# Second mixture of experts: from every expert for every token to blocks of each token's two chosen experts

## The chip, the cores and the metric

The kernel runs on one core of one Trainium2 chip. The metric is the device time of one execution in microseconds (us); the time of a kernel is the median of its runs. A profiled execution, which carries the trace, is a run of its own.

## The reference, cut to what matters

Two transformer layers, each an attention and a mixture of experts, over `x` of 16 rows x 256 tokens x 128 features in float32. After each of the four parts stands `x = layernorm(x + part(x))`. The change touches the last part alone:

```python
def _L1_ffn_ref(x, router_w, w1, w2):        # E = 8 experts, K = 2, H = 512
    logits = einsum('bsd,ed->bse', x, router_w)
    topk_vals, topk_idx = top_k(softmax(logits), K)
    for eid in range(e):
        w = sum(where(idx == eid, vals, 0), axis=-1)
        h = gelu(x_flat @ w1[eid].T)
        y = h @ w2[eid].T
        out = out + w[:, None] * y
```

The weight `w` is zero for the six experts that a token didn't choose. The first layer's mixture (8 experts of 256 and a shared one) has the same form and stays as it is.

## The kernel before

One row (256 tokens, two tiles of 128) is the unit of work. The program is a software pipeline over 18 iterations. Iteration `it` computes stage a of row `it` (first attention, first mixture's up products), stage b of row `it - 1` (first mixture's down products, second attention, router and up products of the second mixture) and stage c of row `it - 2` (gates, down products of the second mixture, last normalization, output). Iterations 0 and 1 and 15 to 17 are written out; 2 to 14 are one hardware loop (`run`, `FIRST`, `LAST`). All weights lie in SBUF from the start. Products that need precision are split in two float32r halves, three products each (`products`).

An iteration has two halves. First the head loop, eight steps `s` of two heads: scores (`score_pair`), their maxima on VectorE (`head_max`, L652), exponent on ScalarE (`softmax_exp`, L544), transposition on TensorE, copy, product with the values, scaling. Then the rest: the output product `OUT`, values of the next row `V0` to `V3`, the transposed row `X1T`, the up products `U0_*` of the first mixture, the end of the second attention (`AOT`, `PROJ`, `X3T`), the next row's `QK0`, `QK1`, and the up products of the second mixture.

The order on TensorE is written by hand in `pe_units(it)`, a list of units with the PSUM bank of each; rings of two or four banks are used in turn. `FILL_B` and `FILL_C` place units of stages b and c between the steps of the head loop. Each unit waits until its bank is drained, and each drain until it is filled. The other engines have their own orders: `body` under `block.scalar`, `block.vector`, `block.gpsimd` and `block.sync`. All engines execute in order.

What the change touches, in its present form:

- `U1_0` to `U1_15` (TensorE, L969 to L971 and L1086) with `gelu1` (ScalarE, L572): x3T times `w1` of every expert, six experts in three split products, two in whole float32. They end the iteration on TensorE; ScalarE loads the exponent's table only behind the last of them.
- `D1e0` to `D1e7` (TensorE, L1101) with `mix` (VectorE, L731): each expert's 512x128 down product, then `x4 = x4 + gate * y`. Six of them stand in the head loop, two behind `OUT`.
- `gate(v, 1, 2)`, `ln_stats` and `ln_apply` of `x4`, and the store of `x4`, all for row `it - 2`.
- `up1`, `up1_whole`, `down1` (SBUF weights, loaded by SyncE) and `split_up_weights(4, ...)` on GpSimd in iteration 0.
- GpSimd's order in an iteration: `rms`, `inverse_std` 1, `head_product`, `value_product`, `inverse_std` 0, 3, 2, `plus`. `plus` frees `x_row`, whose next load SyncE issues at the start of the next iteration; ScalarE squares it at step 1 of the head loop.

## Time and profile before

| | us |
|---|---|
| median of 3 runs (1561.91 to 1562.41) | 1562.2 |
| profiled execution, its own time | 1567.07 |
| its span, first to last instruction | 1565.3 |
| busy: TensorE / VectorE / ScalarE / GpSimd | 1421.9 / 985.5 / 860.9 / 514.5 |
| mean granted TensorE clock, of 1 | 0.976 |

Busy times are sums over instructions. Matmuls are pipelined: each record lasts about 0.28 us while the next starts after 0.12, so the time between starts says what one costs. A product of two whole float32 operands makes two records. The profile's line numbers are those of the kernel above.

### The profile page before, as it was taken

To read this page: it belongs to the slowest core of one execution; us is meant where nothing else is said; L and a number is where in the kernel's file an instruction comes from. 1 tells how busy PE (TensorE), PEld (TensorE's weight loads), DVE (VectorE), ACT (ScalarE), POOL (GpSimd) and SP (SyncE) were. 2 spreads that over 40 slices of the span, in tenths; PEclk is the share of its full clock that TensorE was granted. 3 is DMA by queue.
4 is the path that set the end of the run, shared out by engine and by line. 5 is a ranking of instruction groups with operands and counts; after the bars stand their busy time and mean duration, and the time that the engine had idled before them with its cause. 6 is when DMAs were issued, how large, how long until landed. Compare 5 with 4: busy or idle time off the path is not lost.

```text
span 1565.3 us, 34497 instructions
## 1 busy us (share of the span) xinstructions
PE 1421.9 (91%) x12096; PEld 1249.4 (80%) x12096; DVE 985.5 (63%) x2534; ACT 860.9 (55%) x2361; POOL 514.5 (33%) x415
## 2 busy tenths in 40 slices
PE   6897999999999999999999999999999999998847
PEld 5675888888888888878888888888888887887747
DVE  4456576675757667575666757667575766757482
ACT  5564655656465564647556464655646465463403
POOL 3206061340605134060522506043250614315040
PEclk9898999999999999999999999999999999998978
DMA  7000000000000000000000000000000000000000
GB/s 239 4 2 1 5 2 8 0 7 0 0 7 0 7 0 7 0 0 7 0 7 0 7 0 0 7 0 7 0 1 5 0 7 0 3 1 1 4 1 7
DMA packets 14088, 13.78 MB, mean 9 GB/s; under 512 B 1625, under 2 KB 12770, under 8 KB 13794
## 3 DMA queue, kind: packets, MB, share of 16 engines
q1 hardware_dynamic: 14050, 13.27, 2.6%
q8 instruction: 24, 0.39, 0.1%
q14 instruction: 14, 0.11, 0.0%
HBM read 11.17 MB, written 2.10 MB: 8 GB/s over the span
## 4 chain that ended last, share of the span: by engine, by line
issue 62%; POOL 17%; POOLq 14%; PE 4%; DVE 1%; ACT 1%; DMA 0%; DVEq 0%; SPq 0%
POOLq L329 8%; POOL hid L466 6%; POOL hid L471 6%; POOLq L473 5%; POOL std_inv L427 2%; PE bank_F L1101 1%; POOL up_lo L436 1%; POOL x L488 1%; POOL x_plus L450 1%; POOL rms_inv L443 1%; PE bank_S L983 0%; DMA b_out<-in_b_out 0%; ACT probs L544 0%; DVE hid L743 0%; DVE hid L761 0%
## 5 line engine op out<-in xcount | busy, mean ns | idle before, releaser
L1101 PE MATMUL bank_F<-down,hid 128*128 128x128 f32 x3072 | 374.9, 278 | 34.6 <-DVE x L731 34.0
L1101 PEld LDWEIGHTS bank_F<-down,hid 128*128 128x128 f32 x3072 | 359.4, 193 | 46.3 <-DVE x L731 38.1
L544 ACT ACTIVATE probs<-bank_S,neg_max 128x256 f32<-128x256 f32 x512 | 235.5, 475 | 179.0 <-DVE neg_max L652 178.9
L652 DVE TENSOR_REDUCE neg_max<-bank_S 128x2 f32<-128x512 f32 x256 | 164.6, 684 | 83.5 <-PE bank_S L983 80.2
L471 POOL TENSOR_TENSOR hid<-hid,qkv 128x1024 f32<-128x1024 f32 x62 | 177.1, 2857 | 47.1 <-ACT hid L560 47.1
L731 DVE SCALAR_TENSOR_TENSOR x<-bank_F,gates,x 128x128 f32<-128x128 f32 x512 | 155.2, 345 | 31.6 <-PE bank_F L1101 21.4
L523 ACT ACTIVATE probsT<-bank_T 128x512 f32<-128x512 f32 x256 | 139.6, 605 | 44.1 <-PE bank_T L1012 44.0
L426 POOL TENSOR_TENSOR var_eps<-mv,ln_eps 128x2 f32<-128x2 f32 x64 | 12.5, 195 | 428.5 <-DVE mv L690 428.5
L441 POOL TENSOR_TENSOR mean_sq<-sum_sq,one_over_d 128x2 f32<-128x2 f32 x16 | 3.1, 194 | 455.1 <-ACT h_row L518 455.1
L1012 PE MATMUL bank_T<-ident,probs 128*128 128x128 f32 x1024 | 138.4, 279 | 0.1
L459 POOL TENSOR_TENSOR hid<-qkv 128x1024 f32<-128x1024 f32 x47 | 112.2, 2386 | 66.6 <-ACT qkv L523 66.6
L1040 PE MATMUL bank_A<-probsT,values 128*64 128x256 f32 x1024 | 133.5, 382 | 0.4 <-ACT probsT L523 0.4
L1012 PEld LDWEIGHTS bank_T<-ident,probs 128*128 128x128 f32 x1024 | 113.8, 142 | 23.4 <-issue 21.3
L572 ACT ACTIVATE hid<-bank_T 128x512 f32<-128x512 f32 x141 | 84.2, 598 | 75.5 <-PE bank_T L971 60.4
L466 POOL TENSOR_TENSOR hid<-hid 128x512 f32<-128x512 f32 x77 | 112.8, 1465 | 10.9
L969 PE MATMUL bank_T<-x1T_hi,up_lo 128*128 128x256 f32 x378 | 114.4, 303 | 0.4
L665 DVE TENSOR_TENSOR oT<-oT,bank_A 128x256 f32<-128x256 f32 x128 | 53.6, 419 | 97.0 <-ACT oT L532 95.9
L971 PE MATMUL bank_T<-x1T_hi,up_hi 128*128 128x256 f32 x378 | 107.8, 285 | 0.0
L970 PE MATMUL bank_T<-x1T_lo,up_hi 128*128 128x256 f32 x378 | 107.8, 285 | 0.0
L544 ACT ACTIVATION_READ_ACCUMULATOR probs<-bank_S,neg_max 128x1 f32 x512 | 105.9, 207 | 0.0
L983 PE MATMUL bank_S<-qk_hi,qk_lo 64*128 64x256 f32 x512 | 86.5, 333 | 17.1 <-ACT probs L544 12.5
L572 ACT ACTIVATE hid<-bank_F 128x512 f32<-128x512 f32 x115 | 68.7, 598 | 50.4 <-PE bank_F L971 33.7
(167 smaller groups left out, 3259.1 us busy)
## 6 DMA issues: line engine op xcount, KB each, us to landing
x_row<-in_x SPq DMA_DIRECT2D x16, 128.0 KB, 2.1
down<-in_w SPq DMA_DIRECT2D x1, 2048.0 KB, 14.0
out<-x SPq DMA_DIRECT2D x16, 128.0 KB, 1.8
hid<-in_w SPq DMA_DIRECT2D x1, 1536.0 KB, 7.8
hid<-in_rw SPq DMA_DIRECT2D x1, 1024.0 KB, 6.6
hid<-in_wv SPq DMA_DIRECT2D x1, 512.0 KB, 3.8
hid<-in_wq SPq DMA_DIRECT2D x1, 512.0 KB, 4.7
hid<-in_wk SPq DMA_DIRECT2D x1, 512.0 KB, 5.6
```

The source lines that it names most:

```text
L329: eng.drain()
L466: return g.tensor_tensor(x[:, :, :, 0:n // 2], x[:, :, :, 0:n // 2], x[:, :, :, n // 2:n], ALU.add)
L471: ins = g.tensor_tensor(pv1[:, t, half(i)], *weights_and_values(t, i), ALU.mult)
L523: sc.activation(dst, src, ACT.Copy).then_inc(v.drain(name)[0], 1)
L544: ins = sc.activation(probs[:, h // 2 % 2, h % 2, t, :], unit.bank(f"S{h}")[:, t * S:(t + 1) * S], ACT.Exp, bias=neg_max[:, h, t:t + 1], a ...
L572: sc.activation(hid1[:, e, m:m + 2, :], v.bank(f"U1_{u}")[:, :].rearrange("p (m n) -> p m n", m=2), ACT.Gelu).then_inc(v.drain(f"U1_{u}")[ ...
L652: ve.tensor_reduce(neg_max[:, h, :], v.bank(f"S{h}")[:, :].rearrange("p (t k) -> p t k", t=NT), AX.X, ALU.max, negate=True).then_inc(max_r ...
L731: ins = ve.scalar_tensor_tensor(acc[:, t, :], y[:, j, t, :], gates[i][:, t, e:e + 1], src[:, t, :], ALU.mult, ALU.add)
L969: te.matmul(out, s_lo, m_hi, start=True, stop=False)
L1012: ins = te.transpose(bank[:, k * S + t * P:k * S + (t + 1) * P], probs[:, h // 2 % 2, h % 2, t, tokens(k)], ident[:])
L1040: ins = te.matmul(bank[r, 0:S], values[:, k, s * P + j * DH:s * P + j * DH + DH], probsT[:, j, k, :], start=k == 0, stop=k == NT - 1)
L1101: ins = te.matmul(bank[:, (j * NT + t) * P:(j * NT + t + 1) * P], hid[:, e, k, tokens(t)], down[:, e, k, :], start=k == 0, stop=k == m - 1)
```

## The change

What it does: the second mixture is computed for each token's two chosen experts alone. Rows are taken in five groups (0 to 3, 4 to 7, 8 to 11, 12 to 14, 15). TensorE counts, with a triangular product (`RK`), at which place of its expert each token stands; `place_row` makes two slot numbers of it, and GpSimd scatters the token's normalized features (`x3`) to those two slots of a DRAM buffer `xs[g]`, which has a region of blocks of 128 places for each expert and was filled with zeros. Once the last row of a group is counted (`CN`), `map_blocks` writes on one partition which blocks are used and of which expert: at most 4 x rows + 7 blocks, 23, 19 or 11 a group, and always so many are computed. SyncE reads place and expert of each block into registers and loads the block (64 KB), the expert's `w1` (256 KB) and `w2` (256 KB) into one of eight slots. A block is transposed (`XT`), multiplied with `w1` (`UB`, whole float32), passed through gelu, multiplied with `w2` (`DB`), and stored to its place in `xs[g]`. Once all blocks of a group are stored GpSimd gathers each token's two results, and `combine` adds them to `x3` with their gates; statistics, normalization and store follow. Blocks go in waves (`WAVES`: group, first block, count, iteration of the up product, iteration of the down product). The program is written out whole: no hardware loop.

In the up products nothing is split any more, and `x3` keeps ten rows. The diff, cut to its core:

```diff
-FILL_C = {(2, 1): ["D1e0"], (4, 1): ["D1e1"], (5, 1): ["D1e2"], (6, 1): ["D1e3"], (7, 0): ["D1e4"], (7, 1): ["D1e5"]}
+GROUPS = [range(0, 4), range(4, 8), range(8, 12), range(12, 15), range(15, 16)]
+WAVE_SIZES = [(0, 5, [6, 6, 6, 5]), (1, 9, [6, 6, 6, 5]), (2, 13, [8, 8, 7])]
+WAVES = [(g, sum(sizes[:i]), n, first + i, first + i + 1) for g, first, sizes in WAVE_SIZES for i, n in enumerate(sizes)]
+WAVES += [(3, 0, 8, 16, 16), (3, 8, 8, 16, 16), (3, 16, 3, 16, 16), (4, 0, 8, 17, 17), (4, 8, 3, 17, 17)]
+GATHERS = {9: [0, 1], 10: [2, 3], 13: [4, 5], 14: [6, 7]}
+DOWN_PLACES = [(2, 1), (4, 1), (5, 1), (6, 1)]
...
# fill_units: RK at (0, 0) of stage c, CN at (1, 0) of a group's map iteration,
# DB units at DOWN_PLACES (from iteration 16 on all at (3, 1), then the first XT)
...
# pe_units, iterations of stage a
+        put("F", *[name for w in waves for name, _ in transpose_units(w)])
         put("A", "V0", on=nxt)
         put("G", "V1", on=nxt)
         put("A", "V2", on=nxt)
+        put("G", *blocks[:2])
         put("A", "X1T")
...
         put("A", "V3", on=nxt)
+        put("G", *blocks[2:3])
         put("G", "X3T", on=b)
         put("A", "QK0", "QK1", on=nxt)
+        put("G", *blocks[3:4])
         put("G", "R1", on=b)
+        put("G", *blocks[4:5])
         put("S0", "S0", on=nxt)
         put("S1", "S1", on=nxt)
+        put("G", *blocks[5:])
...
# pe_units, iterations 16 and 17
+    put("G", *up0, *xt1)
+    for i, name in enumerate(dn0):
+        put("G", name, *up1[2 * i:2 * i + 2])
+    if it == ROWS:
+        put("G", "AOT", *xt2, *dn1[:2], *up2, "PROJ", *dn1[2:], "X3T", "R1", *dn2)
+    else:
+        put("G", *dn1)
...
# SyncE
+            def load_blocks(w):
+                g, first, n, up, _ = WAVES[w]
+                if first == 0:
+                    sp.wait_ge(map_ready, g + 1)
+                    sp.wait_ge(scattered[g], 16 * 2 * NT * len(GROUPS[g]))
+                for j in range(n):
+                    place = sp.value_load(block_map[0:1, g, 0, first + j:first + j + 1], ...)
+                    expert = sp.value_load(block_map[0:1, g, 1, first + j:first + j + 1], ...)
+                    # waits until slot j's last block is transposed
+                    sp.dma_start(xb[:, j, :], xs[g][bass.ds(place, 1), :, :]...).then_inc(xb_in[j], 16)
+                for j in range(n):
+                    # waits until slot j's last up product is done
+                    sp.dma_start(w1b[:, j, :], w1_in[bass.ds(expert, 1), :, :]...).then_inc(w1_loaded[j], 16)
...
+                for w in waves_up(v.it):   # in body, behind load_x and zero_fill
+                    load_blocks(w)
+                    if w:
+                        store_blocks(w - 1)
+                    load_down(w)
+                for row in GATHERS.get(v.it - 1, []):
+                    store_row(row)
...
# GpSimd: scatter(row it - 2) ahead of rms; gather(rows) ahead of plus; four each
+            def scatter(v, row):
+                for t in range(NT):
+                    for c in range(2):
+                        g.indirect_dma_start(xs[i]..., bass.IndirectOffsetOnAxis(ap=slots_of[:, row, t, c:c + 1], axis=0),
+                                             x3[:, row % X3_ROWS, t, :], None).then_inc(scattered[i], 16)
...
# VectorE, head loop: place_row at step 0, map_blocks at step 1, gate_row behind gate(v, 1, 2),
# combine(rows gathered in the iteration before) at step 2, combine_norm at step 3
+            def place_row(v):     # nine small instructions
+            def gate_row(v):      # five
+            def map_blocks(v):    # twelve, on one partition
+            def combine(rows):
+                for row in rows:
+                    dve.wait_ge(gathered[i], 16 * 2 * NT * (row // 2 + 1))
+                    for c in range(2):
+                        for t in range(NT):
+                            ins = ve.scalar_tensor_tensor(x[:, t, :], yg[:, i, t, c, :], gates_of[:, row, t, c:c + 1], x[:, t, :], ...)
+                    ln_stats(3 + i, x)
...
# run
-            with eng.Fori(0, LAST - FIRST + 1) as step:
-                body(Iteration(FIRST, step, banks))
+            for it in range(ROWS + 2):
+                body(iteration(it))
```

In iteration 16 ScalarE passes the first wave's blocks through gelu ahead of the second attention's exponent, and VectorE copies that wave's transposed blocks ahead of the second attention's products; the two halves of `gather` for rows 8 to 11 stand between GpSimd's products.

## Rows read from the trace of the kernel before

**Rows 1.** The page: busy time of TensorE; DMA share in 40 slices.
```profile
PE 1421.9 (91%) x12096; PEld 1249.4 (80%) x12096; DVE 985.5 (63%) x2534; ACT 860.9 (55%) x2361; POOL 514.5 (33%) x415
...
DMA  7000000000000000000000000000000000000000
```

**Rows 2.** Timeline of ScalarE, table loads: start us, us, instruction.
```profile
83.09 1.28 ACT L556 ACT_TABLE_LOAD   x1
...
176.84 1.28 ACT L556 ACT_TABLE_LOAD   x1
...
729.76 1.28 ACT L556 ACT_TABLE_LOAD   x1
...
821.93 1.28 ACT L556 ACT_TABLE_LOAD   x1
...
1470.32 1.28 ACT L556 ACT_TABLE_LOAD   x1
```

**Rows 3.** Busy time by stretch: us, PE PEld DVE ACT POOL, granted clock, DMA.
```profile
83.10:175.20 92.10, 77.96 (x643) 66.31 (x644) 58.63 (x147) 52.05 (x144) 30.59 (x23) 0.94 0.01 3
...
639.50:731.70 92.20, 87.12 (x759) 76.78 (x758) 60.37 (x159) 53.23 (x149) 31.65 (x25) 1.00 0.01 3
...
1470.30:1545.00 74.70, 47.55 (x309) 42.78 (x307) 45.52 (x96) 15.26 (x28) 19.78 (x13) 0.79 0.01 2
```

**Rows 4.** Timeline of TensorE, steady iteration.
```profile
715.39 0.36 PE L969 MATMUL bank_T<-x1T_hi,up_lo 128*128 128x256 f32 x1
...
728.95 3.73 PE L1101 MATMUL bank_F<-down,hid 128*128 128x128 f32 x32
...
763.71 1.95 PE L1101 MATMUL bank_F<-down,hid 128*128 128x128 f32 x16
...
765.58 0.39 PE L983 MATMUL bank_S<-qk_hi,qk_lo 64*128 64x256 f32 x2
...
794.85 0.44 PE L953 MATMUL bank_A<-ident,x 128*128 128x128 f32 x2 [1.55 <-DVE x L696]
```

**Rows 5.** Timeline of VectorE, steady iteration.
```profile
734.34 1.29 DVE L652 TENSOR_REDUCE neg_max<-bank_S 128x2 f32<-128x512 f32 x2 [0.57 <-PE bank_S L983]
...
789.06 0.42 DVE L800 TENSOR_TENSOR x<-bank_A,x_plus 128x256 f32<-128x256 f32 x1 [2.37 <-PE bank_A L1025]
...
814.13 1.29 DVE L652 TENSOR_REDUCE neg_max<-bank_S 128x2 f32<-128x512 f32 x2
...
826.50 1.29 DVE L652 TENSOR_REDUCE neg_max<-bank_S 128x2 f32<-128x512 f32 x2 [0.57 <-PE bank_S L983]
```

**Rows 6.** Timeline of VectorE, iteration 1.
```profile
87.39 1.28 DVE L652 TENSOR_REDUCE neg_max<-bank_S 128x2 f32<-128x512 f32 x2
...
91.12 1.29 DVE L652 TENSOR_REDUCE neg_max<-bank_S 128x2 f32<-128x512 f32 x2 [0.16 <-PE bank_S L983]
...
141.92 0.42 DVE L800 TENSOR_TENSOR x<-bank_A,x_plus 128x256 f32<-128x256 f32 x1 [2.44 <-PE bank_A L1025]
...
169.02 1.29 DVE L652 TENSOR_REDUCE neg_max<-bank_S 128x2 f32<-128x512 f32 x2 [0.25 <-PE bank_S L983]
```

**Rows 7.** Groups of instructions by line and form.
```profile
L731 DVE SCALAR_TENSOR_TENSOR x<-bank_F,gates,x 128x128 f32<-128x128 f32 x512 | 155.2, 345 | 31.6 <-PE bank_F L1101 21.4 <-issue 2.2
...
L716 DVE TENSOR_TENSOR marked<-marked,rexp 128x16 f32<-128x16 f32 x32 | 5.6, 175 | 2.4
```

**Rows 8.** SyncE's queue and the DMA list (KB, us to landing).
```profile
12.00 4.16 SPq L360 DMA_DIRECT2D down<-in_sw  x1
...
19.73 0.43 SPq L360 DMA_DIRECT2D down<-in_w  x1
...
x_row<-in_x SPq DMA_DIRECT2D x16, 128.0 KB, 2.1
```

**Rows 9.** Timeline of GpSimd, head sums in the head loop.
```profile
762.92 1.28 POOL L466 TENSOR_TENSOR hid<-hid 128x512 f32<-128x512 f32 x1
...
766.66 2.07 POOL L466 TENSOR_TENSOR hid<-hid 128x512 f32<-128x512 f32 x1
```

More of the change, by code:

```diff
@@ L30 @@
 F32R = mybir.dt.float32r
+I32 = mybir.dt.int32
 ALU = mybir.AluOpType
@@ L45, with n_blocks, region_blocks, space_blocks @@
 LN_EPS, RMS_EPS = 1e-5, 1e-6
-SPLIT1 = 6
-FIRST, LAST = 2, ROWS - 2
+GROUPS = [range(0, 4), range(4, 8), range(8, 12), range(12, 15), range(15, 16)]
+SLOTS = 8
+X3_ROWS = 10
+def n_blocks(g):
+    return 4 * len(GROUPS[g]) + E - 1
+def region_blocks(g):
+    return 2 * len(GROUPS[g])
+def space_blocks(g):
+    return -(-(E * region_blocks(g) + E - 1) // 8) * 8
+def group_of(row):
+    return [g for g, rows in enumerate(GROUPS) if row in rows][0]
+def map_iteration(g):
+    return GROUPS[g][-1] + 2
@@ new lines, in down_units, with up_names, unit_with, earlier @@
+def down_units(w):
+    n = WAVES[w][2]
+    return [(f"DB{w}_{i}", range(2 * i, min(2 * i + 2, n))) for i in range(-(-n // 2))]
+def up_names(w):
+    return [f"UB{w}_{j}" for j in range(WAVES[w][2])]
+def unit_with(units, j):
+    return [name for name, slots in units if j in slots][0]
+def earlier(w, j):
+    return [u for u in range(w) if WAVES[u][2] > j]
+def waves_up(it):
+    return [w for w, wave in enumerate(WAVES) if wave[3] == it]
+def waves_down(it):
+    return [w for w, wave in enumerate(WAVES) if wave[4] == it and wave[3] != it]
@@ new lines, in transformer_blocks @@
+        xb = sb("xb", P, SLOTS, D)
+        xbT = sb("xbT", P, SLOTS, P)
+        yb = sb("yb", P, SLOTS, D)
+        yg = sb("yg", P, 2, NT, 2, D)
+        projections = [w1b[:, 2 * n:2 * n + 2].rearrange("p a h -> p (a h)") for n in range(3)]
+        zeros = hidb[:, 0:2].rearrange("p a k s -> p (a k s)")
+        upper = sb("upper", P, P)
+        one = sb("one", P, 1)
+        first_slot = sb("first_slot", P, 1, E)
+        thresholds = sb("thresholds", 1, 1, MAX_REGION)
+        lower = sb("lower", 1, E, E)
@@ L611, in body @@
                     if v.b and s == 5:
+                        if not v.a:
+                            for j in range(WAVES[waves[0]][2]):
+                                gelu1(v, waves[0], j)
                         head_exp(v, 0)
@@ L617, in body @@
                 sc.activation(table_load[:], table_load[:], ACT.Gelu)
+                if not v.a:
+                    for w in waves[1 if v.b else 0:]:
+                        for j in range(WAVES[w][2]):
+                            gelu1(v, w, j)
+                    return
                 if v.next:
@@ new lines, in combine @@
+            def combine(rows):
+                for row in rows:
+                    i = row % 2
+                    dve.wait_ge(gathered[i], 16 * 2 * NT * (row // 2 + 1))
+                    x = x3[:, row % X3_ROWS]
+                    for c in range(2):
+                        for t in range(NT):
+                            ins = ve.scalar_tensor_tensor(x[:, t, :], yg[:, i, t, c, :], gates_of[:, row, t, c:c + 1], x[:, t, :],
+                                                          ALU.mult, ALU.add)
+                        settled(dve, ins)
+                    ln_stats(3 + i, x)
@@ L817, in fill_out, with combine_norm @@
+            def combine_norm(rows):
+                for row in rows:
+                    ln_apply(3 + row % 2, x3[:, row % X3_ROWS], row // 2 + 1)
             def fill_out(v, s, place):
                 for name in fill_units(v.it, s, place):
+                    if name == "RK":
+                        place_row(v)
+                    if name == "CN":
+                        map_blocks(v)
+                    if name[:2] == "XT":
+                        blocks_transposed(v, int(name[2:].split("_")[0]), [name])
+                    if name[:2] == "DB":
+                        blocks_out(v, int(name[2:].split("_")[0]), [name])
@@ L877, in body @@
                     residual(v, "OUT", x1, x_plus)
-                    ln_stats(v, 0, x1)
+                    ln_stats(0, x1)
+                    for w in waves:
+                        blocks_transposed(v, w)
                 if v.b:
@@ L922, in body @@
                     route(v, 1)
+                if not v.a:
+                    combine(GROUPS[2][2:])
+                    blocks_out(v, waves[2])
+                    combine_norm(GROUPS[2][2:])
                 if v.next:
```

480 lines of the change are left out of this document (364 added, 116 removed).

## The prediction

> **What bounds the kernel now.** I read the page first: TensorE is busy 91% of the span and the DMA engines are idle after the first slice [rows 1], so weights may be fetched again at little cost in the middle of the program. The table loads of ScalarE mark where each iteration begins its head loop [rows 2]: from 729.76 to 821.93 is one period, 92.17 us. The chain of waits is mostly "issue" and says little; the stretches say more. A steady iteration has TensorE busy 87.1 of 92.2 us and VectorE only 60.4 [rows 3]. That looks like a plain TensorE bound, and the second mixture is a large share of it: 64 down products of 128x128 an iteration are 128 records, and 16 records start to start take 765.58 - 763.71 = 1.87 us, 0.117 us each [rows 4], so 15.0 us. The up products are the stretch from 715.39 to 728.95 [rows 4], 13.6 us, of which some 1.4 belong to the router and the next scores.
>
> But one iteration shows how far that reading carries. Iteration 1 runs the head loop without any down unit of the second mixture, because no row is that far yet. TensorE is busy 78.0 us in it, not 87.1 [rows 3], and still the loop's starts lie 176.84 - 83.09 = 93.75 us apart [rows 2]. Read by stages on VectorE: from the first pair of maxima to the residual of the attention output takes 50.8 us there [rows 6], 54.7 in the steady state [rows 5]. So removing six down units (6 x 1.87 = 11.2 us of TensorE) shortens the loop by 3.9 us: the chain scores, maximum, exponent, transposition sets its pace. From the residual to the first maxima of the next row VectorE works nearly without a break, 25.1 us (27.1 in iteration 1, where the granted clock averages 0.94 [rows 3]). And from those maxima to the next loop it takes 12.4 us [rows 5], because ScalarE cannot load the exponent's table before the last up unit; at the start of iteration 1, with no up units ahead of it, the same step takes 3.7 us [rows 6].
>
> **Removed.** The three stages, one by one. The loop: six down units go, three of two blocks each come back (16 records each, as D1e had), in iterations 6 to 15. Half of 3.9 us: 50.8 + 2.0 = 52.8. The new place_row and gate_row add 14 small VectorE instructions, 0.175 us each [rows 7] and about 0.25 with their drains, 3.5 us; they stand in the first two steps of the loop, where VectorE partly waits for scores, and I charge 1.5. That makes 54.3. The second stage: the split copy of X3T and the statistics and normalization of x4 leave VectorE, the copies of the transposed blocks come, but TensorE has an up block ahead of X3T; 25.1 becomes 24.3. The third stage: of the 13.6 us of up products six blocks of 8 records (0.94 us each) remain, two of them ahead of X1T, where TensorE now waits 1.55 us for the normalization [rows 4], and the last one soon after the next scores. The exponent's table can then be loaded before the maxima are there: 3.7 us. The period is 54.3 + 24.3 + 3.7 = 82.3 us. Iterations 1 to 5 carry no down blocks, but may run partly at the lower clock as iteration 1 does; I give them the same. From the start of iteration 1 to that of iteration 16 is 1470.32 - 83.09 = 1387.2 us [rows 2]; 15 x 82.3 = 1234.5. That is -152.7.
>
> **Added inside the loop iterations.** The block map (12 small VectorE instructions in iterations 5, 9 and 13) blocks the queue ahead of the gates and D0p3: about 3.4 us each, of which I charge 2.7: 8 in all. Rows 0 to 7 are combined in iterations 10, 11, 14 and 15: four products of 0.345 us [rows 7] and about as much again in statistics and normalization, 2.8 us a row, of which I charge 2.0: 16. Together +24.
>
> The GpSimd queue: scatters (four indirect DMAs) stand ahead of rms and of the second normalization; gathers (eight in iterations 9, 10, 13, 14) ahead of plus, and so ahead of the next x_row load. No row shows an indirect DMA. Bounds are SyncE's issue, 0.43 us, and its longest, 4.16 [rows 8]. As each works over 128 rows on the same cores I take the nearest GpSimd row, 1.28 us [rows 9]. Scatter: 5.1 us, done about 11 us into the loop; rms waits for squares that come at about 13. Gathers: 10.2 us after the last normalization, when GpSimd is idle for nearly 20 us; plus and x_row (2.1 us [rows 8]) still land before ScalarE squares it. Cost nothing; without this cover, up to 4 x 10 us. The vector engine disturbs GpSimd: the same addition takes 1.28 us alone and 2.07 beside a product of VectorE [rows 9]. The Trainium skill, "SBUF — State Buffer", section "Who interferes with whom", says a DMA issued by GpSimd is starved of descriptors while VectorE copies in its two-port mode (620 ns become 3100 in its example); no run here shows that for a DMA yet, and by its figure a scatter would take some 12 us and be late for rms by about 5.
>
> Traffic: 99 blocks (23, 23, 23, 19 and 11) bring 64 + 256 + 256 KB each and store 64, and 296 places of 64 KB are zeroed in iterations 0 to 4. One x_row of 128 KB lands in 2.1 us [rows 8]; six blocks are 3.8 MB an iteration, some 12 to 20 us of 82 on idle engines [rows 1]. Hidden, as is the zeroing. The gone splitting of the up weights on GpSimd was hidden; the new constants there cost 1 us at the start.
>
> **Straight-line code.** Iteration 1 is already straight-line, and at 93.75 us it is no shorter than the loop's 92.17 [rows 2], which holds a back edge: nothing to win or lose is seen there, and I charge nothing. The Trainium skill, "Runtime: NRT & Kernel Launch", section "Instruction fetch mechanics", says that instructions are streamed in blocks ahead of use and that a taken branch breaks this; by it unrolling could only help, the trace shows no such gain.
>
> **The end.** This is where it gives back. Before, from 1470.32 to the end is 1565.3 - 1470.3 = 95.0 us. Now 30 of the 99 blocks are computed there, one dependent chain behind another, and SyncE's single queue serves them. An issue is 0.43 us [rows 8]; for reading a register from the map no row stands near but that same issue (bounds: nothing, and a DMA's 2.1 us). Per block two reads and four issues (x, w1, w2, store), 6 x 0.43 = 2.6 us; a wave of eight is 20.6 us, 10.3 of them before its last x block is asked for, and one of three 7.7. Walked through from the start of iteration 16: map ready at 12; first wave transposed at 30, behind seven down blocks; its up blocks and table loads put the second attention's exponent back by about 15 us; second wave landed at 47; its down and up blocks to 62; combine rows 8 and 9; AOT at 73, X3T at 84, the last down wave at 97, and only behind it RK of row 15. Then place and four scatters 8, landing 2, eight places read and loaded 12, the rest of SyncE's work and the last down blocks 31, stores 3, four gathers and landing 7, combine, norm and the output 7: 97 + 70 = 167. TensorE is granted 0.79 there already [rows 3]; 30 blocks at half clock would cost 57 us more, I charge 13. So 180 against 95: +85.
>
> **Sum.** -152.7 + 24 + 85 + 1 = -42.7 us against the profiled execution's 1567.07, that is 1524; the median runs are 0.31% below it, so 1520 us. Changes under 0.2% (3 us) can't be told from none.
>
> **Rivals.** (a) The forecast, 1495 to 1545: 0.50. (b) The price of places and row gates is fully hidden (15 x 1.5 = 22 us less) and SyncE's reads are near nothing (60 x 0.43 x 0.8 = 20 less): about 1478. For it: VectorE waits in just those steps; against: four engines take turns there. 0.22. (c) The other side: the end is set by register reads on SyncE. At 2.1 us each, 60 reads cost 60 x 1.67 x 0.8 = 80 us more: 1600. It decides against the change from 1562, that is from 1.3 us a read. For it: they stand in one queue with all loads and stores, nothing overtakes. Against: in waves one and two other waits hide part. 0.20. (d) The iterations gain only what TensorE's idle stages allow and the added DMAs, descriptor starvation or instruction supply costs 3 us in each: 1520 + 45 = 1565, no gain. For it: iteration 1 with 9 us less TensorE work took 93.75 us. Against: its long third stage was the up units, which go. 0.08.
>
> Faster: (a), (b) and part of (d) 0.75; within 0.2%: 0.03; slower: 0.22. The range takes in (b) and most of (c): 1468 to 1592; within (a) alone 1495 to 1545.
>
> **What would show it.** Table loads of the exponent about 82 us apart in iterations 2 to 15; if 88 or more, the third stage did not close. First maxima to the next loop in 4 us. SyncE's issue of eight places in about 10 us; if 20, (c). Iteration 16 and 17 together 180 us; TensorE with about 1,700 records less: a row's second mixture has 72 + 16 up and 128 down records, 3456 in all, against 99 x (1 + 8 + 8) = 1683 and a few for the ranks. The prediction is wrong above all if the walk through the end is off by half, or if the gathers delay x_row.

## The result, and the profile after

The changed kernel took 1616.3 us (median of four runs, 1612.1 to 1618.8) against 1562.3 us for the kernel before beside it: a ratio of 1.033, 95% interval 1.0315 to 1.0346. It is slower, where 1520 us were forecast. The profiled execution took 1612.05 us, its span is 1610.3.

One thing must be said before any row is read. The same program, measured again in three later sets, each beside the kernel before (1564 to 1566 us there), took 1575.2, 1575.8 and 1575.9 us, ratios of 1.005 to 1.007. So two results stand: slower by 3.3% once, by 0.5 to 0.7% three times. Both are slower than before, where faster was forecast. The 41 us between them are followed below, as far as the runs go; their cause stays open. "The control" is the first of the three later ones (experiment 5; its span is 1573.5 us).

The page of the first profile after: busy times and the granted clock in 40 slices; they answer to [rows 1].

```profile
PE 1291.1 (80%) x10473; PEld 1110.6 (69%) x10473; DVE 983.1 (61%) x2660; ACT 776.3 (48%) x2206; POOL 626.6 (39%) x550
PEclk9998998898799999999998888999998899887756
```

TensorE lost 131 us of busy time and 1,623 records, VectorE 2 us. The clock, a 9 almost throughout before, has 8s in the middle and ends at 5 and 6. It is 0.94 on average over iterations 1 to 15 of the control, where it was 0.99 before.

ScalarE's loads of the exponent's table in the first profile after, which answer to [rows 2]: the starts of iterations 1, 9, 10, 11, 12, 16 and 17.

```profile
75.61 1.28 ACT L817 ACT_TABLE_LOAD   x1
757.04 1.28 ACT L817 ACT_TABLE_LOAD   x1
849.91 1.28 ACT L817 ACT_TABLE_LOAD   x1
951.73 1.28 ACT L817 ACT_TABLE_LOAD   x1
1049.16 1.28 ACT L817 ACT_TABLE_LOAD   x1
1418.56 1.28 ACT L817 ACT_TABLE_LOAD   x1
1511.45 1.28 ACT L817 ACT_TABLE_LOAD   x1
```

And the same loads in the control:

```profile
77.66 1.28 ACT L817 ACT_TABLE_LOAD   x1
757.79 1.28 ACT L817 ACT_TABLE_LOAD   x1
845.42 1.28 ACT L817 ACT_TABLE_LOAD   x1
939.17 1.28 ACT L817 ACT_TABLE_LOAD   x1
1029.18 1.28 ACT L817 ACT_TABLE_LOAD   x1
1383.83 1.28 ACT L817 ACT_TABLE_LOAD   x1
1475.62 1.28 ACT L817 ACT_TABLE_LOAD   x1
```

The span falls into three parts, all read from such rows:

| us | before | forecast | first profile | control |
|---|---|---|---|---|
| start to iteration 1 | 83.1 | 84.1 | 75.6 | 77.7 |
| iterations 1 to 15 | 1387.2 | 1258.5 | 1343.0 | 1306.2 |
| iterations 16 and 17 | 95.0 | 180 | 191.7 | 189.7 |

The iterations gained 44 us in the first profile and 81 in the control, where 129 were forecast; the end cost 97 and 95 where 85 were. By the prediction's stages on VectorE, in us: the loop (from the first maxima inside it to the residual of the attention output), from there to the first maxima of the next row, and from those to the next loop's:

| iteration | forecast | first profile | control |
|---|---|---|---|
| 2 | 54.3 / 24.3 / 3.7 | 51.8 / 25.5 / 4.4 | 51.8 / 25.5 / 4.4 |
| 6 | same | 55.6 / 25.2 / 3.7 | 54.0 / 28.2 / 3.7 |
| 8 | same | 54.4 / 24.9 / 3.7 | 54.4 / 24.9 / 3.7 |
| 5 (map) | 57.0 / 24.3 / 3.7 | 59.9 / 24.9 / 4.0 | 59.4 / 24.8 / 4.0 |
| 9 (map, gather) | 57.0 / 24.3 / 3.7 | 57.5 / 28.6 / 6.6 | 57.0 / 24.9 / 4.0 |
| 10 (combine, gather) | 58.3 / 24.3 / 3.7 | 63.6 / 30.8 / 7.8 | 61.9 / 27.9 / 4.1 |
| 11 (combine) | 58.3 / 24.3 / 3.7 | 63.6 / 28.2 / 3.7 | 61.0 / 25.2 / 3.7 |
| 14 (combine, gather) | 58.3 / 24.3 / 3.7 | 64.3 / 29.5 / 5.6 | 62.2 / 24.8 / 5.4 |

The third stage closed as forecast, from 12.4 us to about 4 (5.4 in iterations 13 and 14). In the first profile the second and third stages of the four gathering iterations are long. Iteration 10 there, ScalarE's gelu of the up blocks, then VectorE; in brackets the idle time before an instruction and what ended it:

```profile
940.49 0.60 ACT L832 ACTIVATE hidb<-bank_T 128x512 f32<-128x512 f32 x1 [0.16 <-PE bank_T L1518]
944.82 0.60 ACT L832 ACTIVATE hidb<-bank_F 128x512 f32<-128x512 f32 x1 [3.73 <-remote]
950.62 0.60 ACT L832 ACTIVATE hidb<-bank_T 128x512 f32<-128x512 f32 x1 [5.21 <-remote]
946.30 0.17 DVE L1311 COPY logits<-bank_T 128x16 f32<-128x16 f32 x1 [1.92 <-remote]
950.74 1.29 DVE L922 TENSOR_REDUCE neg_max<-bank_S 128x2 f32<-128x512 f32 x2 [1.03 <-remote]
```

The same four gelus in the control:

```profile
932.70 0.60 ACT L832 ACTIVATE hidb<-bank_T 128x512 f32<-128x512 f32 x1 [0.20 <-PE bank_T L1518]
935.22 0.60 ACT L832 ACTIVATE hidb<-bank_F 128x512 f32<-128x512 f32 x1 [1.93 <-PE bank_F L1518]
936.56 0.60 ACT L832 ACTIVATE hidb<-bank_T 128x512 f32<-128x512 f32 x1 [0.74 <-issue]
938.55 0.60 ACT L832 ACTIVATE hidb<-bank_F 128x512 f32<-128x512 f32 x1 [1.39 <-PE bank_F L1518]
```

In the first profile the third gelu stands at 950.62, though TensorE had its up block done near 944.3; GpSimd issued its eight gathers from 939.18 to 949.02. "remote" as releaser occurs 26 times in that trace, for ScalarE and VectorE alone, each time within 1.8 us of an indirect DMA, and not once in the control's. From residual to loop iterations 9, 10, 13 and 14 take 35.2, 38.6, 35.9 and 35.1 us against 28.9, 32.0, 30.3 and 30.2: 23 of the 37 us between the spans.

### The profile page after: what moved, and what is told of

It reads as the page before. It is cut to its first block and busy times, and to the rows that moved or that the text cites. A ratio compares the mean times of both kernels' runs of the same rounds, so it can differ in the third digit from the quotient of the medians.

```text
span 1610.3 us, 30931 instructions
## 1 busy us (share of the span) xinstructions
PE 1291.1 (80%) x10473; PEld 1110.6 (69%) x10473; DVE 983.1 (61%) x2660; ACT 776.3 (48%) x2206; POOL 626.6 (39%) x550
## 5 line engine op out<-in xcount | busy, mean ns | idle before, releaser
L1484 PE MATMUL bank_F<-down,hid 128*128 128x128 f32 x1024 | 136.6, 293 | 39.3 <-DVE x L1004 24.8
L698 POOL DMA_INDIRECT xs<-x,slots_of x64 | 63.4, 990 | 257.7 <-DVE slots_of L1109 243.1
L1484 PEld LDWEIGHTS bank_F<-down,hid 128*128 128x128 f32 x1024 | 128.8, 206 | 46.2 <-DVE x L1004 29.4
L1407 PE MATMUL bank_T<-ident,probs 128*128 128x128 f32 x1024 | 150.8, 293 | 0.2 <-ACT probs L805 0.2
L935 DVE TENSOR_TENSOR oT<-oT,bank_A 128x256 f32<-128x256 f32 x128 | 53.6, 418 | 101.9 <-ACT oT L793 98.9
L1428 PE MATMUL bank_A<-ident,row_inv 128*64 128x128 f32 x1024 | 84.9, 287 | 33.7 <-DVE oT L935 26.6
L941 DVE TENSOR_TENSOR qk_lo<-bank_A,qk_hi 128x512 fp32r<-128x512 f32 x128 | 87.7, 685 | 9.1 <-ACT qk_hi L798 6.4
L1428 PEld LDWEIGHTS bank_A<-ident,row_inv 128*64 128x64 f32 x1024 | 53.9, 137 | 54.2 <-DVE oT L935 29.6
L1526 PE MATMUL bank_F<-w2b,hidb 128*128 128x128 f32 x672 | 86.1, 284 | 5.1 <-DMA w2b<-in_w 5.1
L1378 PEld LDWEIGHTS bank_S<-qk_hi,qk_lo 64*128 64x128 f32 x512 | 51.3, 192 | 54.0 <-ACT probs L805 26.5
L1526 PEld LDWEIGHTS bank_F<-w2b,hidb 128*128 128x128 f32 x672 | 83.0, 201 | 5.9 <-issue 5.5
```

The lines of the kernel that those rows point to most:

```text
L1378: ins = te.matmul(v.bank(f"S{2 * s + j}")[:, t * S:(t + 1) * S], q[r, s % 2, 0, tokens(t)], k[r, s % 2, 1, :], start=n == 0, stop=n == 2)
L1407: ins = te.transpose(bank[:, k * S + t * P:k * S + (t + 1) * P], probs[:, h // 2 % 2, h % 2, t, tokens(k)], ident[:])
L1428: te.matmul(bank[j * DH:j * DH + DH, S + t * P:S + (t + 1) * P], row_inv[:, s % 2, n:n + 1].broadcast_to([P, DH]), ident[:], start=True, s ...
L1484: ins = te.matmul(bank[:, (j * NT + t) * P:(j * NT + t + 1) * P], hid0[:, e, k, tokens(t)], down0[:, e, k, :], start=k == 0, stop=k == M0 - 1)
L1526: ins = te.matmul(bank[:, (j - slots[0]) * D:(j - slots[0] + 1) * D], hidb[:, j, k, :], w2b[:, j, k, :], start=k == 0, stop=k == M1 - 1)
```

## The experiments

Each set of four (1 to 4, 5 to 8, 9 to 12; the last, 13 and 14, of two) ran on one chip beside the kernel before, which took 1564 to 1566 us in each. Differences are against the control's 1575.2 us where nothing else is said; for 2, 3 and 4 that is a control of another set, on another chip.

**1. The kernel before, written out.**

```diff
-            with eng.Fori(0, LAST - FIRST + 1) as step:
-                body(Iteration(FIRST, step, banks))
+            for it in range(ROWS + 2):
+                body(Iteration(it, 0, banks))
```

> The kernel before, its loop over iterations 2 to 14 written out; nothing else differs. Theory (straight-line code costs nothing): iterations stay at 92.2 us, 1562 us, within 3. Rival (instruction supply is what makes the quiet iterations of the changed kernel 84.5 us where 82.3 were forecast): some 2 us in each of 13 iterations, 1588 us or more.

1565.2 against 1566.2 us, ratio 0.9995 (0.9986 to 1.0005). The page has 97 instruction packets on one queue where the loop had 24, and an iteration is 91.75 us (727.96 to 819.71). Written out, this loop costs nothing.

**2. Plain gathers for rows 0 to 7.**

```diff
+                        if row < 8:
+                            g.dma_start(yg[:, row % 2, t, c, :], xs[i][2 * t + c, :, :])...
+                            continue
                         g.indirect_dma_start(yg[:, row % 2, t, c, :], None, ...
```

> The changed kernel, but GpSimd fetches for rows 0 to 7 four plain blocks of 64 KB with ordinary DMAs where it gathered with indirect ones; same queue, same bytes, same waits (the fetched data are the wrong rows of features, so the output of these rows differs). Theory (an indirect DMA holds up the signals between the other engines while GpSimd works it off): from the residual to the next loop iterations 9, 10, 13, 14 take 35.2, 38.6, 35.9 and 35.1 us; they fall to about 29 to 31, together 20 to 28 us, so 1588 to 1596. Rival (it is DMA traffic, or anything that stands in GpSimd's queue ahead of x_plus): nothing changes, 1611 to 1621.

1575.2 us: 41 below the first measurement, and nothing below the control, which ran only afterwards. Taken alone it would have looked like proof; the next two kernels, which keep all indirect DMAs, showed undisturbed gathers too. So it shows only that indirect gathers cost the iterations nothing beyond ordinary ones in these sets.

**3. No combination of rows 0 to 7.**

```diff
                 for row in rows:
+                    if row < 8:
+                        ve.tensor_copy(stats[3 + i][:, 0, 0:1], yg[:, i, 0, 0, 0:1]).then_inc(stats_ready[3 + i], 1)
+                        continue
```

> The changed kernel without the combination of rows 0 to 7: the eight products, statistics and normalization of these rows are left out, the gathers stay. Theory (this work of VectorE stands fully on the loop's chain): the loops of iterations 10, 11, 14 and 15 fall from 63.6, 63.6, 64.3 and 61.3 us to about 55, together 33 us, so 1583. Rival (2 us a row as forecast, the rest of the long loops comes from the gathers or the clock before them): 16 us, so 1600.

1545.2 us, 30 less. The loops of iterations 10, 11, 14 and 15, 61.9, 61.0, 62.2 and 62.0 in the control, take 54.0, 54.0, 54.0 and 53.6: 31.5 us for eight rows, 3.9 a row. The profiled spans differ by 24.3 us alone, because the second stages of iterations 11, 12 and 13 now take 28 us, at a granted clock of 0.88. The four loops themselves ran at 0.92 to 0.94 in the control and run at 1.00 here, so the 3.9 us a row hold something of the clock's as well. The theory holds for a combination that stands in one piece; what experiment 7 adds is that most of it need not.

**4. Fixed places and experts.**

```diff
-                    place = sp.value_load(block_map[...], ...)
-                    expert = sp.value_load(block_map[...], ...)
+                    place, expert = first + j, (first + j) % E
```

> The changed kernel with SyncE's reads of the block map replaced by fixed numbers: block n of a group is place n of its buffer and expert n modulo 8; waits, bytes and issues stay (the output differs, since places and experts are not the tokens'). Theory (a read is about 0.5 us and hidden except in iterations 16 and 17): 60 reads, some 60% of them on the chain there, 15 to 20 us less, so about 1598. Rival (reads are what makes the end long): 60 us less or more, 1556. Second rival (wholly hidden): 1616.

1556.6 us, 18.6 less; the end is 176.0 us where it was 189.7, and iterations 1 to 15 are as in the control. The other 4.6 us lie ahead of iteration 1 (73.1 us for 77.7), where no map is read. SyncE's queue at the first wave of iteration 16, of the control and then of this kernel (start, duration, count):

```profile
1398.46 12.20 SPq L554 DMA_DIRECT2D xb<-xs  x8
```

```profile
1392.29 3.66 SPq L553 DMA_DIRECT2D xb<-xs  x8
```

Eight issues take 12.20 us with their sixteen reads and 3.66 without: 0.53 us a read. The first theory holds in kind: 60 reads are 32 us, of which the end gives back 13.7, a little less than the theory's 15 to 20. Rival (c) of the prediction, decided at 1.3 us a read, is out.

**5, 9 and 13. The changed kernel again.** No edit.

> The changed kernel itself, unchanged, as a control for the three experiments before, in whose traces no wait ends late beside an indirect DMA although two of them keep all of these. Theory (the late waits of the first profile come with that run and not with the kernel's text): about 1575 to 1580, iterations 9, 10, 13, 14 from residual to loop 29 to 32 us. Rival (they belong to the kernel, and each of the three edits happened to remove them): 1612 to 1621 again, 35 to 39 us.

1575.2 us.

> The changed kernel again, as a second control: it took 1616 us in the first measurement and 1575 in the control, the same program. If it takes about 1575 here (ratio 1.005), the late waits of the first profile are rare and stay a matter of that one run's surroundings; if 1612 to 1620 (ratio 1.03), they come back, and the kernel below without any indirect DMA, run beside it, tells whether these cause them.

1575.8 us, ratio 1.0068 (1.0047 to 1.0089).

> The changed kernel once more, a third control, in another call. 1575 to 1577 and no late wait: then 1616 belongs to the surroundings of the first measurement. 1612 to 1620: then it comes back, and the trace beside it is compared wait by wait.

1575.9 us, ratio 1.0072 (1.0054 to 1.009). The three traces agree in every iteration to 0.2 us, and none has a late wait. 1616 never came back. These controls ran on two chips; the record doesn't say on which the first measurement ran, so that it was a third is not excluded.

**6. The last row dense.** Row 15 leaves the groups; in iteration 17 every expert is computed for it. Nothing of the computation is left out in it, nor in 7, 8, 10, 11 and 14.

```diff
-GROUPS = [range(0, 4), range(4, 8), range(8, 12), range(12, 15), range(15, 16)]
+GROUPS = [range(0, 4), range(4, 8), range(8, 12), range(12, 15)]
...
+        put("G", *[f"UD0_{e}" for e in range(E)])          # iteration 17, tile 0
+        for p, pair in enumerate(DOWN_PAIRS):
+            put("G", f"DD0_{p}", f"UD1_{2 * p}", f"UD1_{2 * p + 1}")
+        put("G", *[f"DD1_{p}" for p in range(len(DOWN_PAIRS))])
...
+            for j in range(E):                             # SyncE: fixed addresses
+                sp.dma_start(w1b[:, j, :], w1_in[j, :, :]).then_inc(w1_loaded[j], 16)
```

> The changed kernel, but row 15 is no group of its own: every expert is computed for it in iteration 17 from the transposed row and weights fetched at fixed addresses (16 up and 16 down blocks where there were 11), with no ranks, scatter, map or gather for it; the gathers of rows 12 to 14 stand together. Theory (the end is long because one dependent chain of rank, scatter, register reads, load and store follows another): iteration 17, 98.9 us before, takes 45 to 55, so 45 to 55 us less than the control. Rival (the end is bound by TensorE's work at its lower clock and by the traffic of the weights): five more blocks and no shorter, within 10 us of the control.

1539.3 us, 36 less; ratio to the kernel before 0.9835 (0.9819 to 0.9852). Iteration 17 takes 63.5 us (1472.7 to the end at 1536.2), not 45 to 55: right in kind, missed in size. The rival is out. Two things went together, though: row 15's own chain, and an order on VectorE. In the control the copy of row 15's last transposed blocks stands behind the combination of rows 12 and 13, and TensorE waits 4.52 us for it; here that copy is gone too.

**7. The combination spread over the steps.**

```diff
-                        combine_norm(GATHERS.get(v.it - 1, []))     # step 3
-                        combine(GATHERS.get(v.it - 1, []))          # step 2
+                    if s >= 1:      # ahead of o_scale: two products, or one row's statistics
+                        combine_part(GATHERS.get(v.it - 1, []), s)
...
-                for row in GATHERS.get(v.it - 1, []):          # GpSimd, behind rms
-                    inverse_out(row)
...
+                    for row in GATHERS.get(v.it - 1, []):      # GpSimd, behind the first products
+                        inverse_out(row)
```

> The changed kernel, but the combination of two rows no longer stands in one piece at step 2 and 3 of the head loop: two products at a time ahead of each scaling of steps 1 to 4, statistics at 5 and 6, normalization at 7. Theory (VectorE idles about 1 us ahead of each scaling, which waits for ScalarE): the loops of iterations 10, 11, 14, 15 fall from 62 to about 57, 15 to 22 us less than the control. Rival (each step's chain takes up whatever VectorE adds, wherever it stands): at most 5 us less.

1574.2 us, 1 less. The loops of iterations 10 and 11 fell by 0.4 and 0.5 us. By its total the rival holds, but not by its mechanism. The loop of iteration 10 in three kernels, us from one pair of maxima to the next, the last from the last pair to the residual:

| | between the seven pairs in the loop | last |
|---|---|---|
| no combination (experiment 3) | 6.5, 7.6, 8.0, 5.6, 7.0, 6.8 | 12.6 |
| control | 6.5, 7.6, 15.0, 7.5, 5.9, 6.8 | 12.6 |
| this kernel | 6.5, 7.6, 8.0, 5.6, 5.9, 7.2 | 20.8 |

Up to the last maxima this loop is as short as one without any combination: eight products and the statistics, spread, cost nothing. They use up VectorE's wait for ScalarE, 1.08 us at these places in the control:

```profile
856.44 0.60 DVE L1184 SCALAR_TENSOR_TENSOR x<-yg,gates_of,x 128x128 f32<-128x128 f32 x2
857.60 0.42 DVE L935 TENSOR_TENSOR oT<-oT,bank_A 128x256 f32<-128x256 f32 x1 [0.56 <-ACT oT L793]
```

All of the 8.2 us stand in the last step, with the normalization at step 7. GpSimd, then VectorE:

```profile
896.62 1.26 POOL L678 TENSOR_TENSOR hid<-hid 128x512 f32<-128x512 f32 x1
897.84 0.19 POOL L638 TENSOR_TENSOR var_eps<-mv,ln_eps 128x2 f32<-128x2 f32 x1
899.83 2.76 POOL L683 TENSOR_TENSOR hid<-hid,qkv 128x1024 f32<-128x1024 f32 x1
898.91 0.60 DVE L966 TENSOR_SCALAR x<-x,mv,std_inv 128x128 f32<-128x128 f32 x2 [2.15 <-POOL std_inv L639]
899.90 3.02 DVE L966 TENSOR_SCALAR x<-x,mv,std_inv 128x128 f32<-128x128 f32 x2 [0.39 <-POOL std_inv L639]
902.85 0.41 DVE L935 TENSOR_TENSOR oT<-oT,bank_A 128x256 f32<-128x256 f32 x1
```

The inverses stand behind GpSimd's head products in this kernel, so VectorE waits 2.15 and 0.39 us for them, and the second row's normalization takes 3.02 us beside a GpSimd product where the first row's took 0.60. The scaling of the heads starts 6.1 us later for it, and from the last scaling to the residual it is 4.9 us at a granted clock of 0.63, where the control has 2.9 at 1.00. In the control the normalization waits too, once for the two rows:

```profile
877.42 2.04 DVE L966 TENSOR_SCALAR x<-x,mv,std_inv 128x128 f32<-128x128 f32 x6 [1.79 <-POOL std_inv L639]
```

Whether the normalization can be hidden as well, at another place or with its inverses earlier, was not tried. The most that it could give is the 30 us of experiment 3.

**8. Both.** The two edits above together.

> The edits of the two kernels before this together. Theory: the gains add, 60 to 75 us less than the control, and the kernel is faster than the one before the change by 3% or more. Rival: one gain hides the other or neither is there, less than 20 us.

1539.9 us, 35 less, as the dense row alone; neither range was hit. The spread combination, 1 us by itself, adds nothing.

**10. Down units late.**

```diff
-DOWN_PLACES = [(2, 1), (4, 1), (5, 1), (6, 1)]
+DOWN_PLACES = [(2, 1), (4, 1), (7, 0), (7, 1)]
```

> The changed kernel with its third and fourth down unit at step 7 of the head loop, (7, 0) and (7, 1), where the kernel before had two, instead of at (5, 1) and (6, 1). In the control TensorE idles about a third of the time from step 6 on to the first products behind X1T, and then its clock is granted at 0.55 to 0.59 for some 7 us (iteration 6: 548 to 572, then 572 to 580). Theory (that thin stretch is what lets the clock fall to 1.2 GHz, and the 2.9 us by which iterations 6, 7 and 10, at 27.9 in their second stage, are longer than 8 and 12, at 24.9, is its price): filled, the dips go where waves are in flight, iterations 6 to 8 and 10 to 15: 10 to 20 us less than the control. Rival (two units there put off the last scaling and OUT by 2 to 3 us in each of them, and the clock does as before): 10 us or more slower. Third: both, no change.

1580.0 us beside a control of 1575.8. None of the three came out pure. Why it was tried: stretches of the control in iteration 6, one of 24 us and then of 4 us (columns: busy us of TensorE, its weight loads, VectorE, ScalarE and GpSimd, then the granted clock, the DMA engines' share and GB/s):

```profile
548.00:572.00 24.00, 17.04 (x140) 13.29 (x139) 18.33 (x36) 10.14 (x25) 15.52 (x9) 1.00 0.22 77
568.00:572.00 4.00, 2.10 (x17) 1.73 (x17) 3.78 (x8) 1.19 (x2) 0.95 (x1) 1.00 0.00 0
572.00:576.00 4.00, 4.00 (x22) 4.00 (x22) 1.90 (x3) 1.68 (x4) 0.00 (x0) 0.55 0.00 0
576.00:580.00 4.00, 4.00 (x24) 4.00 (x23) 0.69 (x2) 2.52 (x6) 0.00 (x0) 0.59 0.00 0
580.00:584.00 4.00, 4.00 (x33) 3.86 (x33) 2.06 (x8) 3.52 (x9) 1.58 (x3) 1.00 0.00 0
```

TensorE works 17 of 24 us, then is granted mostly 1.2 GHz, just when the up products of the first mixture keep it full. The second stage of iterations 7 and 8, in the control and then in this kernel:

```profile
649.51:677.38 27.87, 24.38 (x171) 22.69 (x169) 18.25 (x51) 13.92 (x29) 5.30 (x6) 0.88 0.05 15
735.74:760.62 24.88, 21.96 (x178) 20.38 (x176) 18.27 (x52) 13.78 (x29) 5.31 (x6) 1.00 0.03 7
```

```profile
651.05:675.90 24.85, 21.38 (x171) 19.62 (x169) 18.24 (x52) 13.68 (x29) 5.29 (x6) 1.00 0.16 53
735.12:762.96 27.84, 24.92 (x178) 23.43 (x176) 18.25 (x51) 13.98 (x29) 5.29 (x6) 0.88 0.06 20
```

The same instructions take 24.9 us at a clock of 1.00 and 27.9 at 0.88: that 3.0 us is the clock's is shown. That moving work into the thin stretch keeps the clock up is not: the dip left iterations 7 and 10 and came to 8 and 12. Iterations 1 to 15 are 6 us longer together, most of it because the loops of iterations 6 to 15 each grew by 0.2 to 0.9 us. A neighbouring rival, that these dips depend on how the whole iteration falls in time and not on this stretch, was not tested.

**11. Dense, with three orders changed.**

```diff
-                if v.it == ROWS:                          # SyncE: stores of rows 8 to 11
-                    for row in GROUPS[2]:
-                        store_row(row)
...
             load_dense_down(range(3))
+            for row in GROUPS[2]:
+                store_row(row)
...
+                            if (t, p) == (1, 2):          # VectorE
+                                combine(GROUPS[3][:2])
```

> The kernel with row 15 dense, and three orders changed: SyncE issues the dense weights in iteration 16 ahead of the stores of rows 8 to 11 (it stood 8.7 us in those, and TensorE then waited 4.95 us for w1), rows 12 and 13 are combined between the dense products of row 15 where VectorE waits for TensorE, and GpSimd's inverses follow that order. Theory (weights and stores set the last 50 us): 10 to 15 us less than 1539. Rival (the gathers of rows 12 to 14, done at 1517, set it): 4 us or less.

1532.7 us, 6.6 less than kernel 6; ratio to the kernel before 0.9787 (0.9766 to 0.9808). Iteration 17 takes 54.4 us. That comparison is across two sets; iteration 17 alone is 9.1 us shorter than in kernel 6. Between theory (10 to 15) and rival (4): the three orders together set part of it, and which of them did how much is not told apart. The two last iterations of the control, then of this kernel:

```profile
1383.80:1475.60 91.80, 58.23 (x429) 54.21 (x430) 44.77 (x115) 19.47 (x33) 35.46 (x33) 0.80 0.45 143
1475.60:1573.50 97.90, 40.16 (x256) 37.96 (x254) 29.17 (x120) 9.55 (x16) 25.71 (x34) 0.70 0.36 111
```

```profile
1384.60:1476.10 91.50, 58.81 (x429) 54.79 (x430) 44.81 (x115) 19.44 (x33) 35.46 (x33) 0.79 0.44 143
1476.10:1530.50 54.40, 37.49 (x317) 36.87 (x315) 25.19 (x98) 12.53 (x20) 17.84 (x26) 0.89 0.42 135
```

Iteration 17 has 61 records more and takes 43.5 us less: it was a chain of waits, in which TensorE worked 40 of 98 us.

**12. No indirect DMA.**

```diff
-                        g.indirect_dma_start(xs[i]..., bass.IndirectOffsetOnAxis(...), x3[:, row % X3_ROWS, t, :], None)
+                        g.dma_start(xs[i][4 * (row - GROUPS[i][0]) + 2 * t + c, :, :], x3[:, row % X3_ROWS, t, :])
...
-                        g.indirect_dma_start(yg[:, row % 2, t, c, :], None, xs[i]..., bass.IndirectOffsetOnAxis(...))
+                        g.dma_start(yg[:, row % 2, t, c, :], xs[i][2 * t + c, :, :])
```

> The changed kernel with every indirect DMA replaced by an ordinary one of the same 64 KB on the same queue at a fixed place (the output differs: features land at other places than their tokens'). Theory (in undisturbed runs an indirect DMA costs what any GpSimd DMA costs here): within 5 us of the control beside it, or less by the 1.26 us of an issue where a chain waits for it, in the end: some 10 us. If the control takes 1616, and late waits come from indirect DMAs: 35 us or more below it. Rival then (they come from the traffic, or from anything outside): as late as the control.

1563.9 us, 12 less than its control. The end is 179.6 us instead of its control's 189.8; iterations 1 to 15 are 1302.5 us, 3.6 shorter, all of it in iteration 4 (81.6 us for 85.4), whose loop has less of the low clock. GpSimd's issues of scatters and gathers in iteration 17, in the control and then in this kernel:

```profile
1491.81 1.04 POOL L698 DMA_INDIRECT xs<-x,slots_of  x1 [2.39 <-DVE slots_of L1109]
1493.16 0.97 POOL L698 DMA_INDIRECT xs<-x,slots_of  x1 [0.31 <-issue]
```

```profile
1488.76 2.20 POOL L698 DMA_DIRECT2D xs<-x  x4 [4.18 <-DVE slots_of L1107]
1515.81 4.26 POOL L709 DMA_DIRECT2D yg<-xs  x8 [24.85 <-DMA xs<-yb]
```

An indirect DMA holds GpSimd for 1.27 us (0.97 and 0.30 between), an ordinary one for 0.55.

**14. Each scatter three times.**

```diff
+                        for copy in spare:
+                            g.indirect_dma_start(copy..., bass.IndirectOffsetOnAxis(...), x3[:, row % X3_ROWS, t, :], None)
```

> The changed kernel with each scatter issued three times, the two added ones to DRAM buffers that nobody reads: twelve indirect DMAs ahead of rms where there were four, ten microseconds more on GpSimd at the start of iterations 2 to 17. Theory (indirect DMAs are hidden in the loop iterations, as the forecast had it, and cost only where a chain waits for them): iterations 2 to 15 within 0.5 us each of the control, the end 15 to 20 us longer: 1590 to 1597. Rival (an indirect DMA disturbs the other engines, as in the first profile, only too seldom to be seen with four): waits of ScalarE and VectorE on other engines end late beside them, iterations 2 us or more longer, 1620 or more.

1607.4 us, 31.5 more than its control, between the theory's 1597 and the rival's 1620. The end grew by 19.8 us (209.5), at the theory's upper bound; iterations 1 to 15 by 14, not within 0.5 each: iterations 2, 8 and 12 have 14.1 and iteration 7 gives 2.3 back. These are mostly clock dips: the second stages of 2, 8 and 12 grew by 2.7 to 3.0 us and that of 7 shrank by 3.1; the loop of iteration 2 grew by 3.9 as well. No wait ends "remote". Three times the scatters bring no late wait by themselves.

## Why the prediction was wrong

The sum was 1524 us of a profiled execution. The control's, 1575.2, is 51 us longer, the first one's, 1612.05, 88. Three steps of the prediction failed: the second stage and the clock in it (the period), the discount on the combination, and the walk through iteration 16. The terms, one by one, as the control has them:

- **The period, 82.3 us.** The eight iterations without map or combination average 84.2 us: loop 53.9 (forecast 54.3), second stage 26.2 (24.3), third 4.1 (3.7). 15 x 1.9 = +28 us. That the third stage closes was right. Over all the iterations the second stage is 22.2 us over its forecast, the third 7.4, the passage to iteration 16 4.8, and the plain loops 6.6 under. Of the 22.2, four stages of 27.8 to 28.2 us (iterations 1, 6, 7, 10; granted clock 0.82 to 0.88) make 14.5; iteration 1 had such a dip before the change too. The other ten average 25.1, which is what the stage took before: the 0.8 us a row that were to be won there were not, and make the rest. The loop's good fit is in part luck. Iterations 1 to 5 carry no down blocks, and the loops of 1 and 2 are 51.2 and 51.8 us; but those of 3 and 4 are 55.6, because their first step takes 10.0 us where it takes 6.2 in iteration 2, with TensorE at a granted 0.61. The first step of iteration 2, then of 4:

```profile
168.77:174.97 6.20, 5.78 (x56) 5.32 (x56) 4.16 (x16) 3.99 (x13) 1.26 (x2) 1.00 0.25 98
335.92:345.92 10.00, 10.00 (x60) 9.74 (x62) 4.20 (x17) 4.32 (x13) 3.52 (x4) 0.61 0.06 20
```

  The prediction took TensorE's freed time as a gain or nothing; it gave iterations 1 to 5 a reserve for the lower clock, and did not ask what the thinner work does to the clock in the others.
- **Combination, 2.0 us a row charged.** It measured 3.9, where the work worked out from [rows 7] is 2.8: the step that failed is the discount for waits of VectorE. In one piece the work takes up no wait, and the normalization of each pair of rows waits 1.8 us for GpSimd's inverse besides. That waits of VectorE can take up such work was no bad thought: experiment 7 shows it for the products and the statistics, but only spread over the steps. Charged 16, measured 31.5: +15.
- **The map, 2.7 us each charged.** Iterations 5, 9 and 13 have loops of 59.4, 57.0 and 57.1 against 53.9: 11.8 where 8 were charged, +4. Some 1.6 of the 4 are again the low clock at the first step of iteration 5; against iteration 4 its map costs 3.9 us.
- **Indirect DMAs, nothing in the iterations.** Right (experiments 2 and 12), at the price taken from [rows 9]: 1.28 forecast, 1.27 measured. In the end the walk had charged row 15's scatters and gathers; 40 of the 128 stand there, and ordinary DMAs in their place make it 10 us shorter (experiment 12).
- **The end, 180 us.** 189.7. Register reads at 0.43 us were near (0.53; removing all saves 13.7 in the end). In us from the start of iteration 16, the first wave is transposed at 32 (walk: 30), but the down and up blocks that follow the second wave's landing are done at 72 (62), AOT comes at 82 (73), X3T at 96 (84), the rank of row 15 at 105 (97). From there to the end it is 84.6 us, where the walk had 70 and 13 for the clock: the chain of row 15 was priced nearly right in sum. The walk failed by 8 us in iteration 16, at its second wave, and by 1.6 behind it.
- **Start, +1.** It is 5.4 shorter. The changed kernels have 73.1 to 78.4 us there and the kernel before 83.1 and, written out, 82.4, so this is a gain that the prediction didn't see, not a variation. What of the change gives it was not tested.
- **Straight-line code at nothing.** Right (experiment 1).

28 + 15 + 4 + 10 (the end) - 6 = 51, the miss against the control. Of the rivals, (c) was wrong in its price; (b) did not come, for the reads cost 0.53 us and the iterations ran over the forecast; and (d) was the nearest: its 1565 with the right direction (gains held down in each iteration) and only half its mechanism, for neither the added DMAs nor instruction supply but the clock and VectorE's own work took them. The rule cited there from the Trainium skill, "SBUF — State Buffer", section "Who interferes with whom", by which a DMA issued by GpSimd is starved of descriptors while VectorE copies in its two-port mode, would show as DMAs that take several times as long (in the same page's example, in the section "A bandwidth-pool intuition that's wrong (but worth ruling out)", 3100 ns for 620). The 128 issues of the control, 64 scatters and 64 gathers, average 0.99 and 0.96 us, the longest 1.25. No run here shows it.

**The 37 us more of the first profile** go with waits that end late, seen beside scatters and gathers alone; 23 of them lie in the four gathering iterations, and some of the rest are clock dips, as in the second stage of iteration 11 (28.2 us for 25.2). No step of the prediction had them, and what causes them stays open. Against the indirect DMAs as sole cause: twelve profiles, of ten kernels that keep three quarters of them or more, one with three times the scatters, show none. Against chance within a run: four runs of the first set lie within 7 us. The chip and whatever else surrounded that set remain as rivals, untested: the late waits did not come back, so no experiment on them could be made.

## What to carry to other kernels

Work taken from the busiest engine is worth what its chain gives back: in iterations 1 to 15, 180 us less of TensorE's busy time (1298.9 to the control's 1119.3) became 81 us. Work added to a second engine on that chain costs by how it is placed: in one piece the combination cost its full length and its wait for GpSimd, spread in twos its products and statistics cost nothing, and what then cost 8 us was one normalization whose input another engine delivered late. So when spreading gains nothing in total, look step by step where the time went before calling the work unhideable. A sparse form that pays in the middle of a pipeline may lose at its end, where one dependent chain of rank, scatter, address, load and store has no cover: with the last row computed densely, and the orders that went with it, the kernel is 36 to 43 us shorter, at best 2.1% faster than before (1.9 to 2.3). And before an experiment is read against a first result, run the changed kernel again beside it: experiment 2 would have "proved" a cause by 41 us that the control takes away.

## What the runs showed of the hardware

- One program, on one core at a time, had two levels: 1616 us in one set, 1575 to 1576 in three on two chips, each repeated within its set to 0.5%, with the kernel before at 1562 to 1566 in all of them.
- A granted clock of 0.55 to 0.59 over 8 us of full work, after 24 us of which TensorE had worked 17; such a dip costs 3.0 us where the same instructions can be compared (27.9 and 24.9 us), and which iterations have it changed with small shifts.
- An indirect DMA of 128 rows of 512 bytes holds GpSimd for 1.27 us, an ordinary one of the same bytes for 0.55; reading one number of a map into a register of SyncE takes 0.53.
- Two tiles normalized by VectorE took 0.60 us, and 3.02 beside a GpSimd product that had started 0.07 us before.
